# Row gathers before the norm's powers on GpSimd, in the two combining stages of a four-layer kernel

## The reference, cut to what matters

```python
# layer 0: each token goes to 2 of 8 experts; two shared experts take all tokens
_, idx = jax.lax.top_k(scores + gate_bias, TOPK)
weights = jnp.take_along_axis(scores, idx, axis=1)
for e in range(N_EXPERTS):
    gate_e = jnp.sum(jnp.where(idx == e, weights, 0.0), axis=1)
    h = jax.nn.silu(xt @ w1[e].T) * (xt @ w3[e].T)
    y = y + gate_e[:, None] * (h @ w2[e].T)
z = jax.nn.silu(xt @ sw1.T) * (xt @ sw3.T) @ sw2.T
...
# layer 1: each token goes to 1 of 8 experts
out = x + alpha * ffn
...
x = x + jnp.tanh(g_ffn[0]) * _L0_ffn_ref(_layernorm(x, axis=-1), ...)
x = x + jnp.tanh(g_xattn[1]) * _L1_xattn_ref(_layernorm(x, axis=-1), ctx_1024, ...)
```

## Time and profile before

| what | us |
|---|---|
| median of 3 runs (1390.15 to 1392.39) | 1390.92 |
| the profiled execution, its own time | 1390.4 |
| its span from the first to the last instruction | 1388.7 |
| PE busy (75% of the span) | 1041.1 |
| DVE busy (58%) | 803.3 |
| POOL busy (43%) | 597.8 |
| ACT busy (40%) | 561.4 |

### The profile page before, as it was taken

The page is one execution under the profiler, slowest core; times in us unless marked ns, Lnnn a source line. Parts: engine busy times, 40 slices in busy tenths (PEclk is TensorE's granted clock), DMA queues, the critical chain, the costliest instruction groups (busy, mean ns, idle before and its releaser), DMA issues. The chain is left out here.

```text
span 1388.7 us, 26577 instructions
## 1 busy us (share of the span) xinstructions
PE 1041.1 (75%) x8492; PEld 774.3 (56%) x8493; DVE 803.3 (58%) x1763; ACT 561.4 (40%) x1319; POOL 597.8 (43%) x746
## 2 busy tenths in 40 slices
PE   5777378884558888740799916798887689997998
PEld 3666167883336666630699912455555367776443
DVE  4666154442655877865455545455554538775876
ACT  2462023431126566533334305556552247774000
POOL 1473605565235667657000062556652247763000
PEclk9986589996669999955899966889898789997999
DMA  3463218862041111147777521000000100000000
GB/s 106 119 183 113 87 43 309 289 234 86 29 163 30 36 34 35 35 130 239 254 252 257 193 69 54 1 1 1 0 1 8 39 8 20 16 17 5 16 23 23
DMA packets 70682, 123.47 MB, mean 89 GB/s; under 512 B 15481, under 2 KB 41859, under 8 KB 70595
## 3 DMA queue, kind: packets, MB, share of 16 engines
q1 hardware_dynamic: 63011, 101.64, 22.5%
q0 software_dynamic: 7584, 20.72, 4.4%
HBM read 52.98 MB, written 24.64 MB: 56 GB/s over the span
## 5 line engine op out<-in xcount | busy, mean ns | idle before, releaser
L303 ACT ACTIVATE xnT<-bank 128x256 f32<-128x256 f32 (+1 forms) x112 | 42.2, 381 | 90.7 <-PE bank L292 89.4
L2411 PE MATMUL bank<-l0f_x_high,l_weights 128*128 128x256 bf16 x256 | 51.7, 320 | 34.0 <-issue 20.8
L2820 POOL DMA_DIRECT2D l_results<-keep x23 | 12.5, 544 | 135.3 <-DVE keep L2923 135.3
L3182 PE MATMUL bank<-l_weights,room 128*128 x552 | 65.1, 273 | 4.3 <-DVE room L3210 2.8
L3170 PE MATMUL bank<-room,xnT 128*128 128x128 bf16 x1104 | 67.1, 222 | 0.0
L3170 PEld LDWEIGHTS bank<-room,xnT 128*128 128x128 bf16 x1104 | 65.3, 99 | 0.3
L882 PE MATMUL bank<-ident,l_weights 128*77 128x128 f32 x256 | 39.7, 298 | 33.0 <-DVE l_weights L1073 28.3
L2243 DVE SCALAR_TENSOR_TENSOR l3f_total<-bank,l3f_share,l3f_total 128x256 f32<-128x256 f32 x112 | 54.2, 484 | 15.6 <-PE bank L2161 11.6
L2626 PE MATMUL bank<-room,l0r_placed 128*128 128x128 bf16 x936 | 61.5, 224 | 0.0
L1783 POOL TENSOR_TENSOR l2x_probs<-l2x_probs,l2x_inverse 128x333 f32<-128x333 f32 x64 | 49.5, 796 | 25.4 <-DVE l2x_inverse L1688 25.4
L3182 PEld LDWEIGHTS bank<-l_weights,room 128*128 128x128 bf16 x552 | 52.7, 98 | 12.3 <-issue 5.4
(11 more groups left out here) (430 smaller groups left out, 3252.0 us busy)
## 6 DMA issues: line engine op xcount, KB each, us to landing
xnT<-l_weights SPq DMA_DIRECT2D x23, 1024.0 KB, 5.0
l0r_placed<-l_weights SPq DMA_DIRECT2D x39, 512.0 KB, 3.6
room<-in_L_ffn_weights SPq DMA_DIRECT2D x20, 512.0 KB, 5.0
l0w_staging<-in_L_ffn_weights SPq DMA_DIRECT2D x16, 480.0 KB, 3.8
l_weights<-in_L_ffn_weights SPq DMA_DIRECT2D x16, 384.0 KB, 3.1
room<-l_rows SPq DMA_DIRECT2D x39, 128.0 KB, 3.1
l_results<-room POOLq DMA_DIRECT2D x39, 128.0 KB, 3.1
l_rows<-l_weights SPq DMA_DIRECT2D x16, 184.0 KB, 2.2
```

Of the source, the lines that this page charges most:

```text
L303: act.activation(self.chip.xnT[:, :, span(t, P)], bank[:, 0:DIM].rearrange("p (k n) -> p k n", k=KD), ACT.Copy).then_inc(self.copied, 1)
L2411: last = pe.matmul(self.bank[:, c, branch * width:(branch + 1) * width], self.weights[w][:, at:at + P], x[:, s, k, :], start=(i == 1), sto ...
L3182: last = pe.matmul(bank[:, 2 + u, 0:DIM], h[:, u, c * P:(c + 1) * P], expert_part(split[:, w, :, :], e, KD * hidden_width + c * DIM, DIM), ...
```

## The change

In both layers all gathers are issued first, and the four powers of the norm come behind them.

```diff
-        early = 2
...
         @block.gpsimd
         def _(pool):
-            for g in range(groups + early):
-                for t in range(per * g, min(per * g + per, TILES)):
-                    for k in range(sort.picks):
-                        gather_rows(pool, sort.slot[k], t, targets[k], scratch, gathered[g])
-                if g >= early:
-                    norm.gpsimd(pool, *buffers(g - early)[0], per)
+            for t in range(TILES):
+                for k in range(sort.picks):
+                    gather_rows(pool, sort.slot[k], t, targets[k], scratch, gathered[t // per])
+            for g in range(groups):
+                norm.gpsimd(pool, *buffers(g)[0], per)
```

## The result

| | before | after |
|---|---|---|
| median of 5 runs, us | 1390.15 | 1401.12 |
| lowest and highest, us | 1385.03, 1392.39 | 1392.88, 1405.33 |
| profiled execution, us | 1390.4 | 1400.2 |
| its span, us | 1388.7 | 1398.5 |
| mean granted clock of TensorE in it | 0.859 | 0.849 |

The ratio is 1.0096, with a 95% interval of 1.0061 to 1.0130. The stated range, 1392.5 to 1402.5, is 1.0011 to 1.0083 over the same 1390.92; 1401.12 us lies in it as a time, but the change beside its own kernel before, 1.0096, lies above it. The sign was right and the size too small.

A forecast was written before the change was run, and what follows sets the result against it. Layer 0's stage was taken as held by TensorE and ScalarE crawling beside indirect DMAs, then by VectorE; layer 1's by GpSimd's gathers, then VectorE. -3.97 + 9.0 + 3.1 = +8.1 us on 1390.9 gave 1399.0, range 1392.5 to 1402.5.

The forecast's parts named there:

- The crawl lasts as long as indirect DMAs keep coming: Layer 0's stage: TensorE and ScalarE nearly stop beside gathers, 332 to 355 us, until about 4.6 us behind the last.
- The first rival: Layer 0: the slow stretch ends by itself whatever GpSimd does, price 0, sum -0.9, 1390.0 us; chance 0.14.
- half the price: Layer 0: the slow stretch thins out with time, so the price is 4.5, sum +3.6, 1394.5 us; chance 0.11.
- If the crawl ends 4.6 us behind the last: Layer 0: with the last gather issued 10.1 us later, at 360.3, ScalarE and TensorE return at 365.0, not 354.9.
- the term of +9.0: Layer 0's price: eight moved gathers delay TensorE and ScalarE by 10.1 us, less 1.1 given back; bounds 8.2 and 11.2.
- The given-back part: Layer 0: matmuls done during the slow stretch save time afterwards, about 1.1 us, limited by ScalarE's chain of three chunks.
- the upper bound: Layer 0's price at most 11.2 us, if the return comes 5.7 us behind the last DMA, as with 32 scatters.
- The wait for power 1, -3.97: Layer 0: VectorE's apply of group 1 no longer waits 3.97 us for GpSimd's power behind eight late gathers.
- Layer 0 together: Layer 0's stage: price 9.0 less the vanished wait of 3.97, +5.0 us.
- Layer 1, +3.1: Layer 1's stage: four gathers ahead of power 0 delay apply 0 by 5.0 us; the vanished 1.89 us wait returns some.
- The page against the trace: Layer 0: the skill page says DMAs never contend with compute, so moved gathers cost nothing; the prediction followed the trace instead.
- The rival's price: Layer 0: if the slow stretch ends by itself, moved gathers cost 0 and only the -3.97 us gain remains; chance 0.14.

The follow-up runs named there:

- layer 1 alone: All gathers issued ahead of the powers in layer 1 only, layer 0 in the old order, against the kernel before: ratio 1.0014 (0.9986 to 1.0041).

## Why the prediction was right or wrong

- **The crawl lasts as long as indirect DMAs keep coming.** Right, and now shown downward too (12, 24 and 32 DMAs). The first rival, a crawl that ends by itself, falls: TensorE came back 17.3, 33.9 and 45.1 us after the first gather. So does the second, half the price: the last eight gathers cost 45.13 - 33.85 = 11.3 us, more than their issue. What the first rival had right is the start, which stands behind the same 81st matmul and not at a set time after the first DMA.
- **"If the crawl ends 4.6 us behind the last", the term of +9.0.** This is the step that failed, by its size. The eight gathers were counted at the 1.26 us of GpSimd's issue; the crawl costs 1.41 for each. That is 8 x 1.41 = 11.3 and not 10.1. The given-back part was 0.9 where 1.1 was forecast. Measured at the first add: +10.39. The prediction had the sign of it, 5.7 us behind 32 scatters, and set it aside as the upper bound because the gathers were the nearer row. The better reading of the same rows was per DMA: 33.85 / 24 and 45.4 / 32 agree within 0.01 us.
- **The wait for power 1, -3.97.** Right: it is gone and no other wait took its place. From the first add to line 408 it took 36.03 us before and 32.20 after, -3.83. Layer 0 together: +6.56 where +5.0 was forecast.
- **Layer 1, +3.1.** Right: +2.97, with 5.0 us more of waiting at apply 0 (6.45 against 1.41) and the 1.89 us at apply 1 gone.
- **The sum.** The stages give +9.5 where +8.1 was forecast, and the spans +9.8. The medians of five are 11.0 apart. The last 1.2 us are within what a median of such runs can miss, as the stretch of layer 1's attention alone varies by up to 10 us from run to run; the sets without the crawl, too, have 1 to 3 us more in the times than in the stages, at a lower mean clock. For this no step of the forecast had a term.
- **The page against the trace.** In the execution that was forecast the trace held against the page, and the crawl is real. But in five of seven later sets the trace agrees with the Trainium skill, "SBUF — State Buffer", section "Who interferes with whom", by which a DMA never contends with a compute engine: TensorE did 123 matmuls in 22.8 us beside the same gathers.
- **The rival's price was wrong even where its case holds.** It had layer 0 at -3.97 without the crawl. Measured is about +5. The crawl itself gave power 0 its cover: GpSimd was through with the 24 gathers 23 us before it was wanted. Without the crawl power 0 follows the 24th gather at once, so that eight more gathers in front of it stand on VectorE's path, just as four did in layer 1. The two cases come out close, +6.6 and +5, for different reasons.

## What to carry to other kernels

Before moving issues to the front of an in-order queue, ask what small instruction behind them is waited for, and read the answer with and without the stall that covers it now: here both cases said slower. Size a stall by the count of the things that go with it, over at least two counts, and not by its distance from the last one. Look for its start and its end apart, as they can hang on different things. A stall that the profile puts down to nothing may belong to the session and not to the kernel, so repeat the kernel before on another chip and at another time before tuning against it.

## What the runs showed of the hardware that I had not expected

- The crawl comes and goes with the session. The kernel before takes 1385.62 to 1391.79 us (medians or single runs) where it is there and 1336.89 to 1339.23 where it is not, some 50 us, and layer 0's stage accounts for 83.84 - 60.38 = 23.5 of them. Nearly all of the rest lies beside the scatters: from the first scatter to the first matmul of the experts (line 2833) it is 76.9 us in before and 48.2 in layer 1 alone. Layer 1's stage, where TensorE has only the transposes, doesn't change with it: 38.09 to 38.15 us with the crawl and 37.96 to 38.15 without it in the old order, 41.09 and 41.03 to 41.16 in the new. Each set was of one kind throughout. One and the same chip showed it in one set and not in a later one, so it is no property of the chip. What sets it stays open. Both sets of experiments that had it were those in which each kernel ran only once; the first measurement, with five runs each, had it too.
- Where it is there, TensorE first pauses behind its 81st matmul of layer 0's stage, in all four executions with gathers beside it (9.4 to 11.0 us after the first), and is free 1.41 to 1.44 us per DMA after the first, for rows of 12, 24 and 32. A row of 8, which is issued before TensorE is there, leaves a pause of 0.40 us, and plain copies leave none.
- ScalarE stands too, with all it waits for done: 6.3 us in before and 14.7 in after. So it is not TensorE alone that is held. That something handed out ahead of time, such as a stock of instructions, runs out and is not refilled beside the indirect DMAs would fit both; no run here shows it.
- With the change in layer 0 in place, the mean granted clock of the kernel is lower by 0.003 to 0.007 in every set in which layer 0's part was timed. No run here tells whether the idle time of TensorE in the stage or something else does it.
